# Value products of an attention block issued in runs of two and four head groups, with a fourth slot for the probabilities

## The chip, the core and the metric

The kernel runs on one core of a Trainium2 chip. Its engines work side by side and each takes its own instructions in order: TensorE (PE in the profile, with PEld for its weight loads), VectorE (DVE), ScalarE (ACT), GpSimd (POOL) and SyncE (SP, which issues the DMAs). They wait for one another on semaphores. The metric is the device time of one execution in microseconds (us).

## What is computed

One transformer layer over eight sequences of 256 tokens and width 256: differential attention with 16 heads (two queries a head, so 32 score maps), an added input and a layer norm, then a gated MLP with a router weight, a second added input and a second norm. The part that matters here:

```python
q = jnp.concatenate([q1, q2], axis=1)            # 32 query heads of 16
k2, v2 = jnp.repeat(k, 2, axis=1), jnp.repeat(v, 2, axis=1)
scores = jnp.einsum('bhqd,bhkd->bhqk', q, k2) * scale
p = jax.nn.softmax(jnp.where(causal, scores, finfo.min), axis=-1)
y = jnp.einsum('bhqk,bhkd->bhqd', p, v2)
y = y[:, :H] - sigmoid(x @ Wlam) * y[:, H:]
```

## The kernel before

One iteration handles sequence i of the attention, together with the MLP of sequence i-1 and the end of sequence i-2. The order of each engine's work is written out by hand; nothing reorders it. The first iteration (i = 0) has no MLP in it, the second (i = 1) has no work of sequence i-2, the last (i = 7) has no next sequence to prepare.

The stage that is changed is the one from scores to values. The 32 score maps are split in 8 groups (`GROUPS`). For group g these steps follow one another:

- PE, `t_group(g)` (L746 to L765): three units of transposed scores, u = 0, 1, 2, each into one of four banks (`ring` 0 to 2 and `misc`, taken in turn). A unit waits until the exponentials of the unit four before it are done, since these empty its bank.
- ACT, `exps(g)` (L513 to L518): three exponentials into `prob`, slot g % `RING`, with `RING` = 3. The first one waits, from group 3 on, until the value products that read the slot before are done (`pv_full`).
- POOL, `causal(g)` (L406 to L414): two masks over the slot, one when two exponentials are done, one after the third.
- PE, `pv_group(g)` (L767 to L789): the value products, 16 matmuls of 128*32 in the profile, four next to one another in the columns of the array, into `ybank[g % 2]`. They wait for the masks and for the copy of the group two before.
- DVE, `evacuate_pv(g)` (L1039 to L1041): a copy of the bank to `yv`.

PE's loop in `iteration` issues `t_group(g)`, then for g = 0, 1, 2 a gate/up unit of the MLP (units 4, 5 and 6, `FF_SCORES`; L672 to L674), then from g = 2 on `pv_group(g - 2)`. After the loop come `v_job` (projection of the next values, absent in the last iteration) and `y_jobs` (transposes L800), which wait for the copies to `yv`.

The other engines have MLP work in the same stage. ACT's order is exps(2), tanh of unit 6 (L526), `h_first` of unit 5 (L478), exps(3), `h_first` of unit 6, exps(4), and so on to exps(7). DVE's order is:

```python
for g in range(GROUPS):
    if has_prev and g + 1 in FF_SCORES:
        mlp_unit(i - 1, FF_SCORES[g + 1])
    evacuate_pv(i, g)
    if has_last:
        if g == 0:
            second_norm_start(i - 2, *norm2)
        elif g == SCALE_GROUP + 2:
            second_norm_end(i - 2)
```

So `mlp_unit` of unit 6 (L1030, L1036) stands behind the copy of group 0 and the statistics of the second norm (L999, L1005), and `second_norm_end` (L1126) stands between the copies of groups 5 and 6. POOL has `second_scale` (L386, L388) and the `h_lo` of unit 6 (L403) between the masks of groups 3 and 4.

Two tiles come in with the change. `rest` holds the second half of the split q and k of the next sequence while they are made; `y1` holds the normalized heads, written by DVE after `y_jobs` and read by PE's `yT_job`.

Of the kernel before, what the change touches and what calls it, by code (L numbers as in the profile page):

```python
# [26 lines left out]
B, T, D = 8, 256, 256  # L27
# [10 lines left out]
QK_JOBS = QK_BLOCKS // 2  # L38
# [9 lines left out]
GROUPS = 8  # L48
# [7 lines left out]
LAST_STEPS = 3  # L56
V_COLS = 32
RING = 3
STACKS = 2
X_SLOTS = 3  # L60
REST_SLOTS = 2
HALF = P // 2
# [15 lines left out]
FF_FIRST, FF_MAX, FF_Y0, FF_Y1 = 0, range(1, 4), 7, 8  # L78

FF_SCORES = {0: 4, 1: 5, 2: 6}  # L80
PROJ_CHUNKS = QK_JOBS + 1

SEAM_UNITS = 2
# [4 lines left out]
SCALE = float(HEAD_DIM) ** -0.5  # L88
# [7 lines left out]
ACT = mybir.ActivationFunctionType  # L96
# [3 lines left out]
def build_layer(nc, x, xT, w_proj, w_out, w_gu, w_down, w_router, out):  # L100
    with ExitStack() as ctx:
# [3 lines left out]
        def sem(name):  # L105
# [20 lines left out]
        rest = sb("rest", [P, REST_SLOTS, 2 * T])  # L126
# [7 lines left out]
        max_parts = sb("max_parts", [HEADS * Q_TILES, MAX_PARTS, P], BF16)  # L134
        prob = sb("prob", [P, RING, 3, 2 * T])
        yv = sb("yv", [P, GROUPS, T])

        recip = sb("recip", [P, 3, HEADS])
        y1 = sb("y1", [P, TT, D])
# [9 lines left out]

        gate_t = sb("gate_t", [P, RING, T])  # L150
        h_full = sb("h_full", [P, RING, T])
        h_hi, h_lo = sb("h_hi", [P, FF_UNITS, T], F32R), sb("h_lo", [P, FF_UNITS, T], F32R)
# [14 lines left out]
                     (0, slice(0, yv_cols), yv[:, :, :].rearrange("p g t -> p (g t)")),  # L167
                     (0, slice(yv_cols, gu_cols), mlp_out[:, RING, 0:gu_cols - yv_cols]))

# [30 lines left out]
        qk_full, qk_raw_done, qk_h_done, qk_rest_done, qk_m_done, qk_l_done = (sem(n) for n in ("qk_full", "qk_raw_done", "qk_h_done", "qk_rest_done", "qk_m_done", "qk_l_done"))  # L200
# [4 lines left out]
        t_full, exp_done, causal_done, pv_full, yv_done = (sem(n) for n in ("t_full", "exp_done", "causal_done", "pv_full", "yv_done"))  # L205

        y1_full, y2_full, y1_done, y2_done, y_done = (sem(n) for n in ("y1_full", "y2_full", "y1_done", "y2_done", "y_done"))
        yT_full, yT_hi_done, yT_lo_done, wo_full, z1_done = (sem(n) for n in ("yT_full", "yT_hi_done", "yT_lo_done", "wo_full", "z1_done"))
# [13 lines left out]
        def is_first(b):  # L222
            return b == 0
# [4 lines left out]
        def s_job(u):  # L228
            i, j = S_JOBS[u]
            heads = S_TILE_HEADS[i]  # L230
            return i, range(j * heads, (j + 1) * heads), (i + 1) * HALF

        def t_bank(g, u):
            return score_banks[(3 * g + u) % len(score_banks)]
# [18 lines left out]
        def _(sp):  # L253
# [15 lines left out]
            def load_stacks(b):  # L269
                if b >= STACKS:  # L270
                    sp.wait_ge(t_full, (b - STACKS + 1) * T_UNITS)
                for p in range(3):
# [63 lines left out]
        def _(pool):  # L336
# [69 lines left out]
            def causal(b, groups):  # L406

                for g in groups:
                    first = prob[:, g % RING, 0:2, 0:T].rearrange("p x (i c) -> p x i c", i=2)
                    last = prob[:, g % RING, 2, :].rearrange("p (x i c) -> p x i c", x=2, i=2)  # L410
                    for units, v in ((2, first), (3, last)):
                        pool.wait_ge(exp_done, b * T_UNITS + 3 * g + units)
                        pool.affine_select(out=v, in_=v, compare_op=ALU.is_ge, fill=0.0, base=0,  # L413
                                           pattern=[[0, 2], [HALF, 2], [0, 2], [1, HALF]], channel_multiplier=-1).then_inc(causal_done, 1)  # L414
# [61 lines left out]
        def _(act):  # L476
# [36 lines left out]
            def exps(b, g, units=range(3)):  # L513
                for u in units:
                    act.wait_ge(t_full, b * T_UNITS + 3 * g + u + 1)
                    if u == 0 and g >= RING:
                        act.wait_ge(pv_full, b * GROUPS + g - RING + 1)
                    act.activation(prob[:, g % RING, u, :], t_bank(g, u)[:, :], ACT.Exp, scale=SCALE).then_inc(exp_done, 1)  # L518

            def gate_tanh(b, n):  # L520
                act.wait_ge(gu_full, b * FF_UNITS + n + 1)
# [147 lines left out]
        def _(pe):  # L669
# [76 lines left out]
            def t_group(b, g):  # L746

                rows = slice(0, STACK_ROWS + MAX_PARTS)
                for u in range(3):
                    before = 3 * g + u - len(score_banks)  # L750
                    if before >= 0:
                        pe.wait_ge(exp_done, b * T_UNITS + before + 1)
                    elif g == 0:
                        pe.wait_ge(max_done, b * S_UNITS + S_UNITS - RING + u + 1)
                    else:
                        pe.wait_ge(max_l_done, b + 1)
                    if u < 2:
                        n = 2 * g + u
                        mm = pe.matmul(t_bank(g, u)[:, :], keys_of(b, rows, n, slice(0, P)), q_pair(b, rows, n, slice(0, 2 * T)), start=True, stop=True)  # L759
                    else:  # L760
                        for j in range(2):
                            n = 2 * g + j
                            mm = pe.matmul(t_bank(g, u)[:, j * T:(j + 1) * T], keys_of(b, rows, n, slice(P, T)), q_pair(b, rows, n, slice(T, 2 * T)),  # L763
                                           start=True, stop=True)
                    mm.then_inc(t_full, 1)  # L765

            def pv_group(b, g, has_next):  # L767

                bank = ybank[g % 2]
                if g >= 2:  # L770
                    pe.wait_ge(yv_done, b * GROUPS + g - 1)
                elif has_next:
                    n = (QK_JOBS - 1, 1)[g]
                    pe.wait_ge(qk_raw_done, b * QK_JOBS + n + 1)
                    pe.wait_ge(qk_h_done, (b + 1) * QK_JOBS + n + 1)
                elif g == 0:
                    pe.wait_ge(z1_done, b)
                else:
                    pe.wait_ge(y2_done, b * TT)
                for t in range(TT):  # L780
                    pe.wait_ge(causal_done, b * (2 * GROUPS) + 2 * g + t + 1)
                    for j in range(4):
                        if t == 0:
                            p = prob[:, g % RING, j // 2, :].rearrange("p (i h t) -> p h i t", h=2, t=HALF)[:, j % 2, :, :]
                        else:
                            p = prob[:, g % RING, 2, :].rearrange("p (x i h t) -> p x h i t", x=2, h=2, t=HALF)[:, j // 2, j % 2, :, :]
                        mm = pe.matmul(bank[V_COLS * j:V_COLS * (j + 1), t * P:T], v_ones[:, t, 2 * g + j // 2, :], p,  # L787
                                       start=(t == 0), stop=(t == TT - 1))
                mm.then_inc(pv_full, 1)  # L789
# [119 lines left out]
            def iteration(i, has_next, has_prev, has_last):  # L909
                if i == 2:  # L910
                    pe.wait_ge(mlp_w_lo_done, W_DOWN)
                if not has_prev:
                    first_scores(i)
                for u in range(S_UNITS):
                    if u >= SEAM_UNITS:
                        s_unit(i, u)
                    if has_next and u in QK_AT:
                        qk_job(i + 1, QK_AT.index(u))
                    if has_last and u in SHARED_AT:
                        shared_chunk(i - 2, SHARED_AT.index(u))  # L920
                    if has_prev and u == X1T_AT:
                        x1T_job(i - 1)
                    if has_prev and u == ROUTER_AT:
                        router_job(i - 1)
                    if has_last and u == ROUTED_AT:
                        routed_job(i - 2)
                    if has_prev and u == LOGIT_AT:
                        logit_job(i - 1)
                if has_prev:
                    gu_units(i - 1, (FF_FIRST,))  # L930
                max_job(i, has_prev)
                if has_prev:
                    gu_units(i - 1, FF_MAX)
                pe.wait_ge(max_loaded, (i + 1) * (16 * MAX_PARTS))
                for g in range(GROUPS + 2):
                    if g < GROUPS:
                        t_group(i, g)
                    if g in FF_SCORES and has_prev:
                        gu_units(i - 1, (FF_SCORES[g],))
                    if g >= 2:  # L940
                        pv_group(i, g - 2, has_next)
                if has_next:
                    v_job(i + 1, 0)
                y_jobs(i, 0)
                if has_prev:
                    gu_units(i - 1, (FF_Y0,))
                y_jobs(i, 1)
                if has_prev:
                    gu_units(i - 1, (FF_Y1,))
                yT_job(i)  # L950
                if has_next:
                    v_job(i + 1, 1)
                    first_scores(i + 1)
                wo_job(i)
# [316 lines left out]
```

## Time and profile before

| | before |
|---|---|
| median of 3 runs | 467.77 us (466.49 to 467.85) |
| the profiled execution's own time | 466.94 us |
| its span | 465.2 us, so 1.74 us lie around the span |
| PE busy | 417.3 us, 90% |
| DVE busy | 282.7 us, 61% |
| POOL busy | 244.6 us, 53% |
| ACT busy | 234.9 us, 51% |
| mean granted clock of TensorE | 0.958 |

Shares are means over the whole span. One iteration takes about 51 us; the stage from scores to values is some 17 us of it, and in it the engines are loaded otherwise than in the rest. The chain that ended last is followed back from the last instruction to what released each step, so it shows which engine set the pace where.

### The profile page before, as it was taken

To read this page: it belongs to the slowest core of one execution; us is meant where nothing else is said; L and a number is where in the kernel's file an instruction comes from. 1 tells how busy PE (TensorE), PEld (TensorE's weight loads), DVE (VectorE), ACT (ScalarE), POOL (GpSimd) and SP (SyncE) were. 2 spreads that over 40 slices of the span, in tenths; PEclk is the share of its full clock that TensorE was granted. 3 is DMA by queue.
4 is the path that set the end of the run, shared out by engine and by line. 5 is a ranking of instruction groups with operands and counts; after the bars stand their busy time and mean duration, and the time that the engine had idled before them with its cause. 6 is when DMAs were issued, how large, how long until landed. Compare 5 with 4: busy or idle time off the path is not lost.

```text
span 465.2 us, 10336 instructions
## 1 busy us (share of the span) xinstructions
PE 417.3 (90%) x4008; PEld 339.7 (73%) x4008; DVE 282.7 (61%) x676; ACT 234.9 (51%) x532; POOL 244.6 (53%) x334
## 2 busy tenths in 40 slices
PE   4229697899999999999999999999999999997995
PEld 4127246696799768994998669985898579856995
DVE  3637237753658557764758466755767478747474
ACT  4704481539334853567254944476355922592240
POOL 8314483629355754668254945576365922492152
PEclk9859798979999999999999999999999999999899
DMA  8762770346012810363123610381034410000000
GB/s 284 245 162 63 198 196 2 88 117 151 1 46 85 204 46 4 108 156 69 46 61 108 163 46 25 103 198 33 24 85 112 117 46 0 4 1 25 1 25 23
DMA packets 34753, 40.41 MB, mean 87 GB/s; under 512 B 4240, under 2 KB 28304, under 8 KB 34448
## 3 DMA queue, kind: packets, MB, share of 16 engines
q1 hardware_dynamic: 34704, 39.75, 31.6%
q8 instruction: 32, 0.52, 0.5%
q14 instruction: 17, 0.14, 0.1%
HBM read 27.94 MB, written 11.53 MB: 85 GB/s over the span
## 4 chain that ended last, share of the span: by engine, by line
PE 71%; POOL 9%; DVE 8%; ACT 4%; DMA 3%; issue 2%; SPq 2%; POOLq 0%; DVEq 0%; ACTq 0%
PE ff L672 11%; PE ff L673 10%; PE ff L674 10%; PE ring L735 7%; POOL prob L413 6%; PE ybank L787 5%; PE ybank L672 4%; PE ring L730 4%; PE ring L759 3%; PE ybank L673 3%; PE ybank L674 3%; PE ring L763 2%; ACT prob L518 2%; DVE neg_max L1020 2%; PE ybank L800 2%
## 5 line engine op out<-in xcount | busy, mean ns | idle before, releaser
L1020 DVE TENSOR_REDUCE neg_max<-ring 128x2 f32<-128x512 f32 (+3 forms) x176 | 102.7, 638 | 39.1 <-PE ring L735 38.5
L403 POOL TENSOR_TENSOR h_lo<-h_full,h_hi 128x256 fp32r<-128x256 f32 x72 | 52.9, 735 | 101.6 <-ACT h_hi L478 101.6
L413 POOL TENSOR_SCALAR_AFFINE_SELECT prob<-prob 128x512 f32<-128x512 f32 x128 | 82.9, 679 | 15.6 <-ACT prob L518 14.5
L672 PE MATMUL ff<-x1T_hi,wg_lo 128*128 128x256 f32 x288 | 87.2, 303 | 0.0
L518 ACT ACTIVATE prob<-ring 128x512 f32<-128x512 f32 x144 | 78.3, 620 | 6.9 <-PE ring L759 6.9
L673 PE MATMUL ff<-x1T_lo,wg_hi 128*128 128x256 f32 x288 | 81.2, 282 | 0.0
L674 PE MATMUL ff<-x1T_hi,wg_hi 128*128 128x256 f32 x288 | 81.0, 281 | 0.0
L730 PE MATMUL ring<-mask_b,ident_b 128*128 128x128 bf16 (+2 forms) x176 | 45.4, 258 | 18.9 <-DMA q_stack<-qk_parts_dram 17.1
L1041 DVE COPY yv<-ybank 128x256 f32<-128x256 f32 x64 | 27.0, 422 | 56.9 <-PE ybank L787 56.5
L735 PE MATMUL ring<-k_stack,q_stack 96*128 96x256 bf16 (+3 forms) x512 | 60.9, 239 | 0.0
L787 PE MATMUL ybank<-prob,v_ones 128*32 128x256 f32 (+1 forms) x1024 | 56.3, 335 | 2.0 <-POOL prob L413 1.8
L672 PEld LDWEIGHTS ff<-x1T_hi,wg_lo 128*128 128x128 f32 x288 | 55.0, 191 | 3.3 <-issue 1.3
L526 ACT ACTIVATE gate_t<-ff 128x256 f32<-128x256 f32 x72 | 27.7, 385 | 56.6 <-PE ff L674 56.6
L673 PEld LDWEIGHTS ff<-x1T_lo,wg_hi 128*128 128x128 f32 x288 | 55.1, 191 | 0.0
L674 PEld LDWEIGHTS ff<-x1T_hi,wg_hi 128*128 128x128 f32 x288 | 54.9, 190 | 0.0
L1030 DVE SCALAR_TENSOR_TENSOR gate_t<-gate_t,ff 128x256 f32<-128x256 f32 x72 | 30.0, 416 | 33.5 <-ACT gate_t L526 33.4
L787 PEld LDWEIGHTS ybank<-prob,v_ones 128*32 128x32 f32 x1024 | 25.8, 109 | 29.4 <-issue 9.3
L735 PEld LDWEIGHTS ring<-k_stack,q_stack 96*128 96x128 bf16 x512 | 37.2, 102 | 3.3 <-issue 1.1
L368 POOL TENSOR_TENSOR rest<-rest,parts 128x512 f32<-128x512 f32 x21 | 24.4, 1162 | 28.1 <-ACT parts L478 28.1
L478 ACT ACTIVATE rest<-ybank 128x512 f32<-128x512 f32 x21 | 12.5, 595 | 51.5 <-PE ybank L674 51.5
L730 PEld LDWEIGHTS ring<-mask_b,ident_b 128*128 128x128 bf16 x176 | 17.2, 98 | 27.9 <-issue 17.3
L394 POOL TENSOR_TENSOR parts<-rest,parts 128x512 bf16<-128x512 f32 x24 | 27.8, 1160 | 18.2 <-ACT parts L478 10.2
(169 smaller groups left out, 962.7 us busy)
## 6 DMA issues: line engine op xcount, KB each, us to landing
q_stack<-qk_parts_dram SPq DMA_DIRECT2D x48, 256.0 KB, 4.5
qk_parts_dram<-parts SPq DMA_DIRECT2D x72, 128.0 KB
k_stack<-qk_parts_dram SPq DMA_DIRECT2D x48, 128.0 KB, 4.4
xt_raw<-xT SPq DMA_DIRECT2D x8, 256.0 KB, 2.8
xz<-x SPq DMA_DIRECT2D x8, 256.0 KB, 2.8
out<-xz SPq DMA_DIRECT2D x7, 256.0 KB, 2.2
prob<-w_gu SPq DMA_DIRECT2D x1, 1152.0 KB, 7.3
yv<-w_gu SPq DMA_DIRECT2D x1, 1024.0 KB, 9.1
```

The costliest lines, as they stand in the source:

```text
L394: pool.tensor_tensor(part_order(2, n), psum_order(rest_slot(b, n)), part_order(1, n), ALU.subtract).then_inc(qk_l_done, 1)
L403: pool.tensor_tensor(h_lo[:, n, :], h_full[:, n % RING, :], h_hi[:, n, :].bitcast(F32), ALU.subtract).then_inc(h_lo_done, 1)
L413: pool.affine_select(out=v, in_=v, compare_op=ALU.is_ge, fill=0.0, base=0, pattern=[[0, 2], [HALF, 2], [0, 2], [1, HALF]], channel_multipl ...
L518: act.activation(prob[:, g % RING, u, :], t_bank(g, u)[:, :], ACT.Exp, scale=SCALE).then_inc(exp_done, 1)
L672: pe.matmul(o, lhs_lo, rhs_hi, start=first, stop=False)
L673: pe.matmul(o, lhs_hi, rhs_lo, start=False, stop=False)
L674: return pe.matmul(o, lhs_hi, rhs_hi, start=False, stop=last)
L730: pe.matmul(o[:, :, keys - HALF:keys], ident_b[:, :], mask_b[:, :].unsqueeze(1).to_broadcast([P, len(columns), HALF]), start=True, stop=Fa ...
L735: mm = pe.matmul(o[:, j, :], q_stacks[b % STACKS][rows, row, block, i * P:(i + 1) * P], k_stacks[b % STACKS][rows, row, block, 0:keys], st ...
L787: mm = pe.matmul(bank[V_COLS * j:V_COLS * (j + 1), t * P:T], v_ones[:, t, 2 * g + j // 2, :], p, start=(t == 0), stop=(t == TT - 1))
L1020: dve.tensor_reduce(neg_max[:, columns.start:columns.stop, i], ring[u % RING][:, 0:len(columns) * keys].rearrange("p (h k) -> p h k", k=keys),
L1030: dve.scalar_tensor_tensor(gate_t[:, n % RING, :], gate_t[:, n % RING, :], 1.0, ff[n % 2][:, 0:T], ALU.add, ALU.mult).then_inc(gate_done, 1)
```

## The change

PE's loop issues the value products in three runs: groups 0 and 1 behind the scores of group 3, groups 2 and 3 behind those of group 5, and groups 4 to 7 behind those of group 7. The probabilities get a fourth slot, made of the tile `rest` (the first two units) and the tile `y1` (the third). The first exponential of group g now waits for the value products of group g - 4; in group 3 it also waits until the split of q and k (`qk_l_done`) and the transposes of the sequence before (`yT_full`) are through with the two tiles. The orders of ACT, POOL and DVE stay as they were.

```diff
+PROB_SLOTS = 4
+PV_BEHIND = {3: (0, 1), 5: (2, 3), 7: (4, 5, 6, 7)}
...
+        def prob_first(g):
+            return rest[:, :, :] if g % PROB_SLOTS == RING else prob[:, g % PROB_SLOTS, 0:2, :]
+
+        def prob_last(g):
+            return y1[:, :, :].rearrange("p t d -> p (t d)") if g % PROB_SLOTS == RING else prob[:, g % PROB_SLOTS, 2, :]
+
+        def prob_unit(g, u):
+            return prob_first(g)[:, u, :] if u < 2 else prob_last(g)
...
-                    first = prob[:, g % RING, 0:2, 0:T].rearrange("p x (i c) -> p x i c", i=2)
-                    last = prob[:, g % RING, 2, :].rearrange("p (x i c) -> p x i c", x=2, i=2)
+                    first = prob_first(g)[:, :, 0:T].rearrange("p x (i c) -> p x i c", i=2)
+                    last = prob_last(g).rearrange("p (x i c) -> p x i c", x=2, i=2)
...
-                    if u == 0 and g >= RING:
-                        act.wait_ge(pv_full, b * GROUPS + g - RING + 1)
-                    act.activation(prob[:, g % RING, u, :], t_bank(g, u)[:, :], ACT.Exp, scale=SCALE).then_inc(exp_done, 1)
+                    if u == 0 and g >= PROB_SLOTS:
+                        act.wait_ge(pv_full, b * GROUPS + g - PROB_SLOTS + 1)
+                    if u == 0 and g == RING:
+                        act.wait_ge(qk_l_done, min(b + 2, B) * QK_JOBS)
+                        if not is_first(b):
+                            act.wait_ge(yT_full, b)
+                    act.activation(prob_unit(g, u), t_bank(g, u)[:, :], ACT.Exp, scale=SCALE).then_inc(exp_done, 1)
...
-                            p = prob[:, g % RING, j // 2, :].rearrange("p (i h t) -> p h i t", h=2, t=HALF)[:, j % 2, :, :]
+                            p = prob_unit(g, j // 2).rearrange("p (i h t) -> p h i t", h=2, t=HALF)[:, j % 2, :, :]
...
-                            p = prob[:, g % RING, 2, :].rearrange("p (x i h t) -> p x h i t", x=2, h=2, t=HALF)[:, j // 2, j % 2, :, :]
+                            p = prob_last(g).rearrange("p (x i h t) -> p x h i t", x=2, h=2, t=HALF)[:, j // 2, j % 2, :, :]
...
-                for g in range(GROUPS + 2):
-                    if g < GROUPS:
-                        t_group(i, g)
+                for g in range(GROUPS):
+                    t_group(i, g)
                     if g in FF_SCORES and has_prev:
                         gu_units(i - 1, (FF_SCORES[g],))
-                    if g >= 2:
-                        pv_group(i, g - 2, has_next)
+                    for pv in PV_BEHIND.get(g, ()):
+                        pv_group(i, pv, has_next)
```

## Rows read from the trace of the kernel before

**Rows 1.** Busy us (instructions) by stretch: PE, PEld, DVE, ACT, POOL; clock, DMA, GB/s.

```profile
209.90:220.83 10.93, 10.59 (x150) 4.70 (x149) 5.73 (x15) 8.65 (x19) 9.73 (x16) 1.00 0.26 62
220.83:254.70 33.87, 33.29 (x310) 31.36 (x307) 25.01 (x62) 13.64 (x33) 14.82 (x17) 1.00 0.22 65
```

**Rows 2.** Chain that ended last, iteration 3: start, us, what.

```profile
215.34 4.41 POOL prob L413 x7
219.89 1.01 PE ybank L787 x16
```

**Rows 3.** Timeline of PE, iteration 3: start, us, instruction, idle before and its releaser.

```profile
209.69 0.28 PE L674 MATMUL ff<-x1T_hi,wg_hi 128*128 128x256 f32 x1
209.90 0.86 PE L787 MATMUL ybank<-prob,v_ones 128*32 128x256 f32 x16
210.69 0.60 PE L759 MATMUL ring<-q_stack,k_stack 98*128 98x512 bf16 x2
211.13 0.38 PE L763 MATMUL misc<-q_stack,k_stack 98*128 98x256 bf16 x2
211.44 0.86 PE L787 MATMUL ybank<-prob,v_ones 128*32 128x256 f32 x16
...
214.43 0.39 PE L763 MATMUL ring<-q_stack,k_stack 98*128 98x256 bf16 x2
...
220.83 0.39 PE L672 MATMUL ring<-wp_hi,xt_lo 128*128 128x272 f32 x1
...
221.68 1.03 PE L800 MATMUL ybank<-ident,yv 128*128 128x128 f32 x8
```

**Rows 4.** Timeline of PE's weight loads, iteration 0, one run and two runs together.

```profile
62.81 0.59 PEld L787 LDWEIGHTS ybank<-prob,v_ones 128*32 128x32 f32 x16 [0.21 <-DVE yv L1041]
...
64.36 1.24 PEld L787 LDWEIGHTS ybank<-prob,v_ones 128*32 128x32 f32 x32 [0.21 <-DVE yv L1041]
```

**Rows 5.** Timeline of DVE, iteration 3.

```profile
210.82 0.42 DVE L1041 COPY yv<-ybank 128x256 f32<-128x256 f32 x1 [1.61 <-PE ybank L787]
...
212.53 0.42 DVE L1036 SCALAR_TENSOR_TENSOR h_full<-gate_t,ff 128x256 f32<-128x256 f32 x1
...
218.76 0.42 DVE L1041 COPY yv<-ybank 128x256 f32<-128x256 f32 x1 [1.12 <-PE ybank L787]
...
220.48 0.90 DVE L1041 COPY yv<-ybank 128x256 f32<-128x256 f32 x2
```

**Rows 6.** Timeline of ACT, iteration 3.

```profile
210.29 0.41 ACT L478 ACTIVATE h_hi<-h_full 128x256 fp32r<-128x256 f32 x1
211.12 1.09 ACT L518 ACTIVATE prob<-ring 128x512 f32<-128x512 f32 x2 [0.42 <-PE ring L759]
...
212.98 0.42 ACT L478 ACTIVATE h_hi<-h_full 128x256 fp32r<-128x256 f32 x1 [0.29 <-DVE h_full L1036]
213.31 1.56 ACT L518 ACTIVATE prob<-ring 128x512 f32<-128x512 f32 x3
214.74 0.61 ACT L518 ACTIVATE prob<-misc 128x512 f32<-128x512 f32 x1
```

**Rows 7.** Timelines of DVE, ACT and PE, iteration 1.

```profile
110.09 0.42 DVE L1036 SCALAR_TENSOR_TENSOR h_full<-gate_t,ff 128x256 f32<-128x256 f32 x1
...
111.35 1.59 ACT L518 ACTIVATE prob<-ring 128x512 f32<-128x512 f32 x3
...
118.64 0.39 PE L672 MATMUL ring<-wp_hi,xt_lo 128*128 128x272 f32 x1
```

**Rows 8.** Timelines of DVE and PE, iteration 7.

```profile
420.72 0.90 DVE L1041 COPY yv<-ybank 128x256 f32<-128x256 f32 x2
...
421.27 1.12 PE L800 MATMUL ybank<-ident,yv 128*128 128x128 f32 x8
```

**Rows 9.** Busy time by stretch, end of iteration 7 (columns as in rows 1).

```profile
425.90:429.30 3.40, 1.34 (x10) 0.89 (x9) 2.27 (x6) 1.59 (x4) 1.46 (x2) 1.00 0.00 0
429.30:432.70 3.40, 3.40 (x18) 3.40 (x17) 1.37 (x3) 0.00 (x0) 0.00 (x0) 0.50 0.00 0
```

## The prediction

> **What bounds the kernel now.** I read the page first: PE is busy 90% of the span, the others 51 to 61%. That is a mean over unlike stages, so I went to the busy time by stretch. From the first transposes of one iteration to the last gate/up unit before the values of the next, PE is busy 33.29 of 33.87 us, and in the stage of the change 10.59 of 10.93 [rows 1]. Both look like PE. The chain of waits corrects this for the stage: seven masks of POOL follow one another there without a gap, 4.41 us, and the last value products start when the last mask is through [rows 2]. So PE runs ahead, waits a little at the end, and the pace is set by ACT and POOL, which hand over group by group. The timelines of the single engines then show who waits: ACT has a gap of 0.42 us before exps(3), until the scores of group 3 come from PE, and one of 0.29 us before the `h_hi` of unit 6, until DVE has made `h_full` [rows 6]. DVE itself has waited 1.61 us for the value products of group 0 [rows 5]. These two gaps decide the change. What follows the stage is full of PE, so a delay of the stage goes on to the end undiminished.
>
> **The change part by part.** I take iteration 3 as the pattern of iterations 2 to 6.
>
> *Fewer switches on PE.* A run of value products occupies PE for 0.79 us until the next scores start (209.90 to 210.69) [rows 3]; of two runs back to back the weight loads span 1.24 us against 0.59 for one, so the second costs 0.65 [rows 4]. The way back to full-width scores is thus 0.14 us. Scores take 0.75 us (210.69 to 211.44), and their units follow at 0.22, three of them 0.66, so the way in is 0.09 [rows 3]. Before there are six runs, afterwards three: 3 x 0.23 = 0.7 us of PE an iteration goes away. The Trainium skill, TensorEngine Tiling (Array Packing), section Key Properties, says that a change of tiling mode drains TensorE; the trace agrees with 0.23 us a run. What that page would make of the change stands with the rivals.
>
> *Scores of group 3 ahead of the value products of group 0.* PE is free for them at 209.81 (209.90 less the way in) instead of 210.69. ACT is free at 210.29 + 0.30 = 210.59 (an `h_hi` holds it 0.3: 212.98 to 213.31), so exps(3) starts at 210.59 instead of 211.12: ACT gains 0.53 us [rows 3, 6]. But pv_group(0) now starts 0.75 us of scores after 209.81, at 210.56: 0.66 later.
>
> *Who stands behind pv_group(0).* DVE's copy of group 0 starts 0.92 us after it (209.90 to 210.82), so at 211.48. Behind it in DVE's order stand the norm statistics and `mlp_unit` 6; `h_full` is done at 212.95 now (212.53 + 0.42), then at 213.61 [rows 5]. Behind that, in ACT's order, stand the `h_hi` of unit 6 and all of exps(4): the `h_hi` goes from 212.98 to 213.64, exps(4) from 213.31 to 213.97 [rows 6]. ACT is through with exps(3) at 210.59 + 3 x 0.48 = 212.03 (0.48 is the pitch, 213.31 to 214.74 for three), so it stands 1.6 us where it stood 0.29. The 0.53 is lost, and 0.66 more.
>
> *Scores in pairs.* The second unit of group 5 needs the bank that the first exponential of group 4 empties. A bank is free about 0.64 us after its exponential starts (213.79 to 214.43) [rows 3, 6], so the second unit goes at 214.6 and the third, one pitch on, at 215.09. PE, back at scores at 210.56 + 0.65 + 0.79 = 212.00, is through with those of group 4 at 212.66 and with the first unit of group 5 at 212.88; it stands idle 1.7 us and, before the third unit, 0.25 more. pv_group(2), long ready, stands behind these units; it starts at 215.09 + 0.31 = 215.40. The run of two takes 0.65 + 0.79, so the scores of group 6 start at 216.84, and exps(6) 0.43 us later (210.69 to 211.12) at 217.27. ACT was through with exps(5) at 213.97 + 6 x 0.48 = 216.83: another 0.44 lost. The last unit of group 7 waits for the second exponential of group 6 (217.27 + 0.48 + 0.64 = 218.40), and the run of four starts 0.31 later, 218.71. Four times 0.65 end at 221.31; 0.12 for the copy of group 4, which the third waits for, and 0.14 of way back put `v_job` at 221.57. Before it was 220.83: +0.75 us.
>
> *The tail on DVE.* The copy of group 5 starts at 218.71 + 0.65 + 0.92 = 220.28 (now 218.76); `second_norm_end` follows, so that the copy of group 6 comes 1.72 later, at 222.00 (now 220.48) [rows 5]. The transposes of `y_jobs` need that copy. In iteration 7 they start 0.55 behind it [rows 8]; so at 222.55, where `v_job` alone (0.85) would allow 222.42. Before: 221.68 [rows 3]. The delay is 0.87, and 0.92 in their second half, which needs the copy of group 7. I take 0.9 for each of iterations 2 to 6.
>
> *The other iterations.* In iteration 1 there are no norm statistics: `h_full` goes from 110.51 to 111.17, exps(4) from 111.35 to 111.52, +0.17. From exps(4) to `v_job` it is 118.64 - 111.35 = 7.29 us [rows 7]; by the steps above 221.57 - 213.97 = 7.60. Together +0.5. In iteration 7 no `v_job` covers the copies, so the whole 1.52 us of the copy of group 6 shows: +1.5 [rows 5, 8]. In iteration 0 no MLP work holds up ACT: it gains up to 0.5 from the early scores and loses 0.3 to the pairs; I take 0.
>
> *At nothing.* The new waits of exps(3) are for work that ended in the stages before (POOL's third parts, the transposes of the last sequence); behind it stands all of ACT, but nothing is late. exps(7) waits for pv_group(3) instead of pv_group(4): earlier. No DMA is issued or moved, and SP's order is untouched. Exponentials and masks of groups 3 and 7 use `rest` and `y1`: the trace has no such row. The lower bound is no cost, since shape and engine are the same; the upper is that each exponential takes its whole 0.61 us instead of the pitch of 0.48 [rows 6], where group 3 has cover and group 7 has not: 3 x 0.13 x 8 = +3 us. I take nothing, because the shape is the same. POOL, 0.63 a mask against 0.72 for half of ACT's group, follows ACT; its last mask starts about 220.5, and is over just as the second half of pv_group(7) wants it (221.2).
>
> *Sum.* 0 + 0.5 + 5 x 0.9 + 1.5 = +6.5 us. The profiled execution took 466.94, so 473.4; the median of the runs is 0.83 above it, which makes 474.3 us.
>
> **Rivals.**
>
> A. *PE is the bound after all* (faster). For it: 10.59 of 10.93 us busy [rows 1]. If every unit of scores finds its bank free, the three runs saved pay: 0.7 x 8 = 5.5 us less, 462.3 us. It decides from the point where exps(4) starts no later than 213.3; then the 0.53 us that exps(3) gains must also not be lost at the `h_hi`. Against it: a row already shows ACT waiting there for DVE. The Trainium skill's rule on drains, taken alone, forecasts this case. Chance 0.07.
>
> B. *It comes out even*. The delay at exps(4) is made up, because the copy of group 0 is not what holds DVE, or because POOL gave back what PE loses; the pairs then cost 0.3 in seven iterations less what exps(3) gains, 0 to +1.3 us, 468 to 469. Nothing in the timelines speaks for it but that the first order had 0.3 us of waiting for POOL at its end. Chance 0.07.
>
> C. *The gap on PE also costs clock* (slower still). At the end of iteration 7 PE was busy 1.34 of 3.40 us, and in the next 3.40 us the granted clock was 0.50 of full, 1.2 instead of 2.4 GHz [rows 9]. By my steps PE would be busy about 1.4 us from 212.4 to 215.8. Half the clock for 3.4 us of full work costs at most 1.7. If it falls in two of the five iterations, +3.4: 477.7 us. Against it: the gap is 1.7 and 0.25 us, not one long one, and part of what follows waits for ACT anyway. Chance 0.15.
>
> **Numbers.** The forecast has 0.71: 474.3 us, for itself from 471 (0.4 an iteration and 1 in the last, less than the steps give) to 477 (the 3 us of the tiles' upper bound). With C the range goes to 479; A and B, 0.14, stay below it. Low 470.5, high 479. One measurement of this kernel tells about 0.3% (1.4 us) from no change. Faster 0.07, same 0.07, slower 0.86.
>
> **What would show it.** In iterations 2 to 6: exps(3) earlier by half a microsecond; ACT idle about 1.6 us before the `h_hi` of unit 6, released by DVE `h_full`; PE idle about 1.7 us between the first and second unit of group 5, released by ACT; exps(6) waiting about 0.4 for PE; `y_jobs` behind the copy of group 6; 0.9 us more an iteration; three runs of weight loads at 0.65 a group. If PE is not idle in group 5, A or B holds; if the granted clock of the stage is below 1.00, C does. The prediction is wrong if DVE reaches `mlp_unit` 6 without having waited for the copy of group 0, or if time lost in the stage comes back in the 33.87 us behind it.

## The result and the profile after

The changed kernel takes 474.55 us (median of 4 runs, 473.43 to 478.63), the kernel before 467.81 (4 runs, 466.49 to 469.47). The ratio over the runs is 1.0168, 95% interval 1.0131 to 1.0206; the two medians alone give 1.0144. Ratios here and below go by all runs, save in run 4, where three of six runs that lay over 1.5% above its fastest are left out. The forecast was 474.3. The profiled execution has a span of 471.7 us, 6.5 more than before, at a mean granted clock of 0.954.

The sum is met more closely than its terms. So here is the stage by itself, from the first scores of group 0 to the first transposes of `y_jobs`, the difference of two starts in PE's timeline, for each iteration, in us.

| iteration | 0 | 1 | 2 | 3 | 4 | 5 | 6 | 7 | sum |
|---|---|---|---|---|---|---|---|---|---|
| before | 15.59 | 17.44 | 18.10 | 18.11 | 18.11 | 18.11 | 18.11 | 17.45 | 141.0 |
| after | 15.50 | 17.99 | 20.03 | 18.90 | 18.91 | 18.90 | 20.14 | 18.58 | 148.9 |
| difference | -0.09 | +0.55 | +1.93 | +0.79 | +0.80 | +0.79 | +2.03 | +1.13 | +7.9 |
| forecast | 0 | +0.5 | +0.9 | +0.9 | +0.9 | +0.9 | +0.9 | +1.5 | +6.5 |

All that lies outside these stages is 1.4 us shorter than before. The end alone is 1.6 us shorter: from the transposes of iteration 7 on it takes 42.3 us instead of 43.9. Between the stages nothing of the loss comes back: from the transposes of iteration 3 to the scores of iteration 4 it is 32.96 us before and 33.00 after.

Iteration 3 after, PE's timeline (start, us, instruction, idle before and its releaser). The iteration begins at 205.95 instead of 203.57, so 2.38 us are to be taken off when it is set beside the forecast.

```profile
205.95 0.61 PE L774 MATMUL ring<-q_stack,k_stack 98*128 98x512 bf16 x2
...
212.94 1.51 PE L802 MATMUL ybank<-prob,v_ones 128*32 128x256 f32 x32
214.38 0.60 PE L774 MATMUL ring<-q_stack,k_stack 98*128 98x512 bf16 x2
...
215.04 0.38 PE L774 MATMUL misc<-q_stack,k_stack 98*128 98x512 bf16 x1
216.98 0.39 PE L774 MATMUL ring<-q_stack,k_stack 98*128 98x512 bf16 x1 [1.56 <-ACT prob L533]
217.47 0.39 PE L778 MATMUL ring<-q_stack,k_stack 98*128 98x256 bf16 x2
...
221.12 2.26 PE L802 MATMUL ybank<-prob,v_ones 128*32 128x256 f32 x48
...
224.00 0.39 PE L687 MATMUL ring<-wp_hi,xt_lo 128*128 128x272 f32 x1
```

Two runs of value products now stand together (x32) and take 1.44 us until scores follow, where one took 0.79 [rows 3]. Then PE is idle for 1.56 us before the second unit of group 5, and the releaser is ACT. `v_job` comes at 224.00, less 2.38 at 221.62, where it came at 220.83.

ACT in the same stretch:

```profile
212.97 1.08 ACT L533 ACTIVATE rest<-ring 128x512 f32<-128x512 f32 x2
...
216.03 0.42 ACT L489 ACTIVATE h_hi<-h_full 128x256 fp32r<-128x256 f32 x1 [1.49 <-DVE h_full L1050]
216.35 1.55 ACT L533 ACTIVATE prob<-ring 128x512 f32<-128x512 f32 x3
...
219.66 0.60 ACT L533 ACTIVATE prob<-ring 128x512 f32<-128x512 f32 x1 [0.29 <-PE ring L774]
```

The gap of 0.42 before exps(3), which write `rest` here, is gone; the one before the `h_hi` of unit 6 has grown from 0.29 to 1.49 us [rows 6], released by DVE's `h_full`; and before exps(6) there is a new one of 0.29, for PE.

DVE in the same stretch:

```profile
213.87 0.42 DVE L1055 COPY yv<-ybank 128x256 f32<-128x256 f32 x1 [2.27 <-PE ybank L802]
...
215.57 0.42 DVE L1050 SCALAR_TENSOR_TENSOR h_full<-gate_t,ff 128x256 f32<-128x256 f32 x1
...
222.70 0.42 DVE L1055 COPY yv<-ybank 128x256 f32<-128x256 f32 x1 [0.23 <-PE ybank L802]
223.04 1.01 DVE L1140 TENSOR_SCALAR xz<-xz,ln_mv,ln_t 128x256 f32<-128x256 f32 x2
223.97 0.74 DVE L1055 COPY yv<-ybank 128x256 f32<-128x256 f32 x2
```

It stands 2.27 us before the copy of group 0, where it stood 1.61 [rows 5]: the 0.66 that pv_group(0) is later. The chain that ended last no longer goes through POOL's masks in this stage [rows 2] but through just this:

```profile
213.01 0.83 PE ybank L802 x16
213.87 0.42 DVE yv L1055
214.29 0.67 DVE ln_stats L1013 x2
...
215.57 0.43 DVE h_full L1050
...
216.83 0.60 ACT prob L533
```

The stages of iterations 2 and 6, at 20 us, are something else. Busy time by stretch (columns as in rows 1): iterations 3 and 6 of the kernel after; two stretches inside its iteration 2; and the two stretches behind iteration 7 that lie as far behind its transposes as those of [rows 9] did, in the second of which the clock was at half before.

```profile
206.04:224.94 18.90, 17.10 (x204) 11.18 (x204) 8.21 (x22) 14.77 (x33) 15.06 (x24) 1.00 0.46 116
361.87:382.02 20.15, 18.49 (x204) 11.83 (x204) 8.21 (x23) 14.78 (x33) 15.11 (x24) 0.92 0.44 110
...
162.40:165.84 3.44, 1.78 (x27) 0.98 (x31) 1.02 (x4) 2.84 (x7) 2.94 (x5) 0.99 0.01 4
165.84:169.25 3.41, 3.41 (x22) 1.17 (x14) 0.70 (x2) 2.52 (x7) 2.17 (x4) 0.51 0.00 0
...
434.03:437.43 3.40, 1.38 (x11) 0.93 (x10) 2.21 (x6) 1.59 (x4) 1.45 (x2) 1.00 0.00 0
437.43:440.83 3.40, 3.40 (x33) 3.40 (x32) 1.70 (x5) 0.00 (x0) 0.39 (x2) 1.00 0.00 0
```

The same 204 matmuls take PE 1.4 us longer in iteration 6, at a mean clock of 0.92. In iteration 2 the clock is at 0.51 of full, so at 1.2 instead of 2.4 GHz for nearly all of it, in the stretch that follows PE's gap. And the half clock behind iteration 7 did not come in this execution: 33 matmuls pass in the 3.40 us in which 18 passed before. That is the 1.6 us that the end gained.

### The profile page after: what moved, and what is told of

Read it like the earlier page. It is cut to its first block, busy times and chain, and to the rows that moved or that the text cites. A ratio compares the mean times of both kernels' runs of the same rounds, so it can differ in the third digit from the quotient of the medians.

```text
span 471.7 us, 10336 instructions
## 1 busy us (share of the span) xinstructions
PE 412.1 (87%) x4008; PEld 340.0 (72%) x4008; DVE 278.2 (59%) x676; ACT 234.8 (50%) x532; POOL 246.0 (52%) x334
## 4 chain that ended last, share of the span: by engine, by line
PE 73%; DVE 11%; ACT 6%; DMA 3%; issue 3%; SPq 2%; POOL 1%; POOLq 0%; DVEq 0%; ACTq 0%
PE ff L687 11%; PE ff L688 10%; PE ff L689 10%; PE ybank L802 9%; PE ring L750 7%; ACT prob L533 4%; PE ring L745 4%; PE ybank L687 3%; PE ring L774 3%; PE ybank L689 3%; PE ybank L688 3%; PE ring L778 2%; DMA q_stack<-qk_parts_dram 2%; DVE neg_max L1034 2%; PE ybank L815 2%
## 5 line engine op out<-in xcount | busy, mean ns | idle before, releaser
L424 POOL TENSOR_SCALAR_AFFINE_SELECT prob<-prob 128x512 f32<-128x512 f32 x96 | 62.8, 678 | 18.8 <-ACT prob L533 17.0
L533 ACT ACTIVATE prob<-ring 128x512 f32<-128x512 f32 x112 | 62.0, 609 | 7.9 <-PE ring L774 7.9
L774 PE MATMUL ring<-q_stack,k_stack 98*128 98x512 bf16 x96 | 34.8, 406 | 13.4 <-ACT prob L533 10.0
L802 PE MATMUL ybank<-prob,v_ones 128*32 128x256 f32 (+1 forms) x768 | 37.4, 332 | 0.0
```

The costliest lines, as they stand in the source:

```text
L533: act.activation(prob_unit(g, u), t_bank(g, u)[:, :], ACT.Exp, scale=SCALE).then_inc(exp_done, 1)
```

## The experiments

Each kernel was timed in turns with the kernel before on the same chip; the medians of before lay between 467.89 and 468.48 us.

**1. Unit 6 ahead of the copy, in the changed kernel.** One edit on DVE:

```diff
-                    if has_prev and g + 1 in FF_SCORES:
-                        mlp_unit(i - 1, FF_SCORES[g + 1])
+                    if has_prev and g == 0:
+                        for n in (FF_SCORES[1], FF_SCORES[2]):
+                            mlp_unit(i - 1, n)
                     evacuate_pv(i, g)
```

> The changed kernel with one thing moved on DVE: unit 6 of the MLP ahead of the copy of group 0. Theory (the loss is DVE's unit 6, and with it ACT's exps(4), queued behind the copy of the late value products): exps(4) starts about 1.5 us earlier, PE's gap in group 5 goes, the stage of iterations 3 to 5 shrinks from 18.9 to about 17.6 us (18.11 before the change), and the time is about 465 us, below the kernel before. Rival (the pairs and their banks hold PE, wherever DVE stands): stage at 18.7 or more, 473 us. Rival (the clock lost in PE's gap is the loss): only the two slow iterations recover, about 472 us.

Measured: 464.65 us, ratio to before 0.9935 (0.9910 to 0.9959). The stages of iterations 2 to 6 take 17.54 or 17.55 us, all five, against 18.90 with the change and 18.11 before. DVE's timeline in iteration 3 of this kernel:

```profile
211.66 0.42 DVE L1050 SCALAR_TENSOR_TENSOR h_full<-gate_t,ff 128x256 f32<-128x256 f32 x1
212.27 0.42 DVE L1055 COPY yv<-ybank 128x256 f32<-128x256 f32 x1 [0.19 <-PE ybank L802]
```

ACT's timeline behind it:

```profile
212.80 0.44 ACT L489 ACTIVATE h_hi<-h_full 128x256 fp32r<-128x256 f32 x1
213.21 1.58 ACT L533 ACTIVATE prob<-ring 128x512 f32<-128x512 f32 x3
```

And PE's, the first two units of group 5:

```profile
213.44 0.38 PE L774 MATMUL misc<-q_stack,k_stack 98*128 98x512 bf16 x1
213.86 0.39 PE L774 MATMUL ring<-q_stack,k_stack 98*128 98x512 bf16 x1
```

DVE has made `h_full` while it would have waited, ACT goes from exps(3) to exps(4) without a gap, and PE issues the second unit of group 5 0.42 us behind the first instead of 1.94. The same runs on PE, the same pairs, and the sign of the change turns. The theory holds; both rivals fall.

The edit takes unit 6 past the copy and also past the norm statistics behind it. Iteration 1 of the changed kernel has no statistics, and there ACT's gap is 0.57 us instead of 1.49, and the stage loses 0.55 instead of 0.79:

```profile
111.02 0.42 ACT L489 ACTIVATE h_hi<-h_full 128x256 fp32r<-128x256 f32 x1 [0.57 <-DVE h_full L1050]
```

Run 3 below, without the pairs, loses 0.28 in that iteration. So the late copy alone is enough for a loss, and what else stands between the copy and unit 6 adds to it.

**2. The same edit in the kernel before.**

> The kernel before with the same move on DVE alone. Theory: there the h_hi of unit 6 waited only 0.29 us and POOL's masks set the end of the stage, so nothing changes: stage 18.1 us, 467.8 us. Rival (any gain of the first run is simply the better order on DVE): about 465 us here too.

Measured: 467.89 us, ratio 0.9999 (0.9975 to 1.0023), stages of 18.12 us. The chain that ended last goes through POOL's masks in iteration 3, as in the kernel before:

```profile
217.55 4.42 POOL prob L413 x7
```

The better order on DVE is worth nothing here by itself; it is needed only once the value products are late.

**3. Late, but one by one.** The changed kernel with

```diff
-PV_BEHIND = {3: (0, 1), 5: (2, 3), 7: (4, 5, 6, 7)}
+PV_BEHIND = {3: (0,), 4: (1,), 5: (2,), 6: (3,), 7: (4, 5, 6, 7)}
```

> The changed kernel with runs of one: groups 0 to 3 one by one behind the scores of groups 3 to 6, groups 4 to 7 behind group 7. The lateness of group 0 is kept, the pairs are undone. Theory (lateness is most of it, pairs the rest): stage of iterations 2 to 6 about 0.6 us above the kernel before, 472 us. Rival (the pairs are the loss): 467.8 us. Rival (drains are worth their 0.23 us a run): two runs more than the changed kernel, so slower than it, 475 us or more.

Measured: 471.82 us, ratio 1.0098 (1.0063 to 1.0133). The undisturbed stages take 18.63 us: 0.52 above before, and 0.27 below the changed kernel. So lateness is two thirds of the 0.79, the pairs one third (the last run of four is the same in both). Iteration 4 took 20.20, with a clock of 0.92 in its stage. PE of iteration 3 shows the same gap, a little shorter, between the first two units of group 5:

```profile
213.00 0.39 PE L774 MATMUL misc<-q_stack,k_stack 98*128 98x512 bf16 x1
214.71 0.39 PE L774 MATMUL ring<-q_stack,k_stack 98*128 98x512 bf16 x1 [1.32 <-ACT prob L533]
```

**4. Both edits.**

> Both edits: runs of one, one group late, and unit 6 first on DVE. Theory: the early scores of group 3 now pay and nothing is queued behind the late copy; iterations 2 to 6 gain 0.5 us each against the kernel before until POOL's masks hold the end, 464.5 us, as much as the first run or a little more, although there are two more runs on PE. Rival (drains): 0.5 us an iteration slower than the first run.

Measured: a median of 465.23 us (459.11 to 466.28), ratio 0.9869 (0.9812 to 0.9926). The stages say it more plainly: 17.58 us, against 17.54 in the first run. The chain that ended last, iteration 3 of this kernel:

```profile
211.45 3.78 POOL prob L424 x6
215.23 0.64 POOL rest L424
...
216.00 1.01 PE ybank L802 x16
```

Two runs of value products more on PE, 0.46 us by [rows 3, 4], make no difference here: POOL's masks end this stage. That is less than a proof that switches are free, since run 1 ends otherwise: its chain goes through ACT's exponentials and through PE's run of two (1.44 us) and run of four (3.03), with no mask of POOL in it. The two stages come out alike with different ends. The rival that puts the weight on the drains falls for run 4. What the Trainium skill states in TensorEngine Tiling (Array Packing), Key Properties, that a change of mode drains the array, is not touched by this. The 0.23 us a run are there in PE's rows, only not on this path.

**5. The fourth slot alone.** The new tiles and waits, with PE's order as before (`PV_BEHIND = {2: (0,), 3: (1,), 4: (2,), 5: (3,), 6: (4,), 7: (5, 6, 7)}`).

> The order of the kernel before on PE (runs as they were), with the fourth slot in the other two tiles and the new waits. Theory: the tiles and the waits cost nothing, stage 18.1 us, 467.8 us. Rival (exponentials and masks in the other tiles are dearer, up to 0.4 us an iteration): 468 to 471 us, stage 18.2 to 18.5.

Measured: 467.78 us, ratio 0.9998 (0.9974 to 1.0022), stages of 18.11 to 18.12 us. The tiles and the waits cost nothing that the stage shows.

**6. PE's gap filled.** The changed kernel with spare products, whose results are thrown away, behind the first unit of group 5:

```diff
+                    if g == 5 and u == 0 and not is_first(b):
+                        pe.wait_ge(yv_done, b * GROUPS + 1)
+                        for _ in range(12):
+                            pe.matmul(ybank[0][:, 0:T], wg_hi[:, 0, 0:P], x1T_hi[:, 0, :], start=True, stop=True)
```

> The changed kernel with twelve spare matmuls of 256 columns (1.4 us, results thrown away) in PE's gap between the first and second unit of group 5, from iteration 1 on. Theory (the gap makes the clock fall in some iterations): no iteration at half clock in the stage, 18.9 us in all of iterations 2 to 6 instead of up to 20.1, about 0.8 us more in iteration 1 whose gap is shorter, 472 to 473 us with less scatter than the changed kernel. Rival (the two slow iterations have nothing to do with the gap): slow iterations of 20 us stay, 474 us or more. Rival (the gap is not idle for want of ACT): the spare matmuls push the stage out by up to 1.4 us, 480 us.

Measured: 474.76 us, ratio 1.0158 (1.0126 to 1.0190). Iterations 2 to 6 took 18.92, 18.91, 18.86, 18.91 and 18.91: no stage at a lower clock in this execution, and none of the five pushed out by the spare work. PE's timeline in iteration 3 of this kernel, the spare matmuls and the second unit of group 5:

```profile
214.35 1.76 PE L784 MATMUL ybank<-x1T_hi,wg_hi 128*128 128x256 f32 x12
216.27 0.39 PE L774 MATMUL ring<-q_stack,k_stack 98*128 98x512 bf16 x1
```

The time as a whole is not clearly shorter: iteration 1 pays 0.34 more, iteration 7 had the half clock behind it again (43.9 us from its transposes to the end), and the runs scatter as before. My 472 to 473 was too low.

**7. The changed kernel a second time.**

> The changed kernel as it is, a second look. Theory (whether the clock falls in PE's gap depends on where the gap lies in time, not on the iteration): undisturbed stages of 18.9 us again, with stages near 20 us in other iterations than 2 and 6, or in another number of them; time 473 to 478 us, as that number goes. Rival (iterations 2 and 6 are slow for a reason of their own): the same two at 20 us.

Measured: 476.53 us (6 runs), ratio 1.0173 (1.0144 to 1.0202). Undisturbed stages of 18.9 again, and about 20 now in iterations 3, 6 and 7. Busy time by stretch, iterations 3 and 4:

```profile
205.50:225.50 20.00, 18.34 (x204) 11.90 (x203) 8.14 (x23) 14.78 (x33) 15.15 (x24) 0.91 0.44 111
258.50:277.40 18.90, 17.11 (x204) 11.16 (x203) 8.28 (x23) 14.78 (x33) 15.17 (x24) 1.00 0.46 117
```

So it is not the iteration. Over all the profiled executions here, a full iteration (2 to 6) fell to a lower clock in 5 of 15 stages with the gap open (the changed kernel twice, and run 3), in none of the 35 in which the gap was not there, and in none of the 5 in which it was filled. Five stages are few: at one in three, all five stay clear by luck in one case of eight. The clock of the other executions says more. With the gap filled, the mean granted clock was 0.954 or 0.958 in all 5; in the changed kernel it was 0.945 to 0.948 in 7 of 10. So the idle time itself is likely what costs the clock; the total time does not show it.

**8. POOL's item last.** Run 4, and on POOL the `h_lo` of unit 6 behind the last mask:

```diff
-                    if has_prev and g - 1 in FF_SCORES:
+                    if has_prev and g - 1 in FF_SCORES and g < 3:
                         n = FF_SCORES[g - 1]
                         h_rests(i - 1, range(n, n + 1))
                 if has_prev:
-                    h_rests(i - 1, range(FF_Y0, FF_UNITS))
+                    h_rests(i - 1, range(FF_SCORES[2], FF_UNITS))
```

> Runs of one, one group late, unit 6 first on DVE, and on POOL the h_lo of unit 6 behind the last mask instead of between the masks of groups 3 and 4. Theory (POOL's 0.68 us there hold the masks, and through them the end of the stage): stage of iterations 2 to 6 at about 17.2 us, 462 us, below the fourth run. Rival (ACT holds the end already): 17.6 us, as the fourth run.

Measured: 461.03 us, ratio 0.9832 (0.9794 to 0.9870): the fastest of all by its median, 7.2 us below that of before in the same rounds. Stages of 17.03 us, a little shorter than forecast. POOL's timeline in iteration 3 of this kernel, with the masks straight behind the scale of the second norm, 10.51 us into the stage where they came at 11.18 in run 4:

```profile
214.41 0.71 POOL L399 TENSOR_TENSOR ln_t<-ln_t,minus_half 128x2 f32<-128x2 f32 x1
215.08 3.82 POOL L424 TENSOR_SCALAR_AFFINE_SELECT prob<-prob 128x512 f32<-128x512 f32 x6
```

The busy time of that stage (columns as in rows 1):

```profile
204.57:221.60 17.03, 17.03 (x204) 11.14 (x203) 8.56 (x23) 14.56 (x33) 15.01 (x24) 1.00 0.56 133
```

PE is busy for all of the 17.03 us, and the chain that ended last holds nothing but PE from the scores of group 3 on. In iteration 3 of every other kernel here the chain leaves PE for ACT, DVE or POOL; here, and only here, PE is the bound of the stage. Whether the three runs of the change would pay here was not run.

**9. The two moves without the change.** The kernel before with the edits of runs 1 and 8.

> The kernel before with the two moves on DVE and POOL and nothing of the change. Theory: with POOL's item out of the way the old order gains too, but keeps its late scores of group 3: stage 17.5 us, 464.5 us, between the kernel before and the run with the scores early. Rival (the gain of the early scores was POOL's all along): the same 17.2 us as that run.

Measured: 464.02 us, ratio 0.9924 (0.9895 to 0.9953), stages of 17.52 us. Of the 1.08 us that run 8 gains in an iteration, 0.59 come without the change, and 0.49 with the later value products. In iteration 3 of run 9 ACT still waits for the scores of group 3, and the chain goes from there through POOL's masks:

```profile
210.68 1.08 ACT L518 ACTIVATE prob<-ring 128x512 f32<-128x512 f32 x2 [0.42 <-PE ring L759]
```

So most of the 0.49 is what the early scores save. The later value products also make one run less, which is not on this chain.

## Why the prediction was right, and where only the sum was

**The stall.** Taken 2.38 us back, the steps of iteration 3 lie where they were put: exps(4) at 213.97 (forecast 213.97), the run of two at 215.41 (215.40), the scores of group 6 at 216.85 (216.84), exps(6) at 217.28 (217.27), the run of four at 218.74 (218.71), `v_job` at 221.62 (221.57). ACT's gap was 1.49 us where 1.6 was forecast, PE's 1.56 where 1.7 was, and the wait of exps(6) 0.29 where 0.44 was. All three were forecast a little too long because I let an engine be free one pitch after its last instruction started (0.48 on ACT, 0.22 on PE), while that instruction itself takes 0.61 or 0.38 [rows 3, 6]; the starts, which carry the sum, do not depend on it. (For exps(6) there is a slip besides: 213.97 + 6 x 0.48 is 216.85, not 216.83.) Run 1 shows that this is the cause and not only the order in which things happened: with `mlp_unit` 6 off the queue behind the copy, the loss of 0.79 becomes a gain of 0.57. Run 3 shows the split between lateness and pairs.

**The tail was too dear.** I took 1.72 us from the copy of group 5 to that of group 6, as before [rows 5]; it took 1.27, because `second_norm_end` took 1.01 us instead of 1.46. Its row before, for the one shown above:

```profile
219.11 1.46 DVE L1126 TENSOR_SCALAR xz<-xz,ln_mv,ln_t 128x256 f32<-128x256 f32 x2
```

So the copies are not what `y_jobs` waits for in iterations 2 to 6, `v_job` is: 0.79 instead of 0.9 each. In iteration 7 the term was 1.13 instead of 1.5. Undisturbed, the stages add up to -0.09 + 0.55 + 5 x 0.79 + 1.13 = 5.54 us, not 6.5.

**The clock made up for it.** What rival C described came as well, in two of five iterations, as in its example: +1.1 and +1.2 us, less than the 1.7 each that I had as the most. At the end the half clock of before was missing, 1.6 us less. These three and +0.2 us elsewhere make +0.94, and the forecast total is met by that. It is luck of this execution: in the profiled execution of run 7 three stages fell and the end was at half clock too, and the median of that run was 476.53. The likeliest case and C should not have been set apart as they were; with a gap of 1.3 to 1.6 us the clock fell in 5 of 15 stages.

**The rest.** The tiles and waits at nothing: right (run 5). POOL off the path in the changed kernel: right, the chain has none of its masks in the stages of iterations 1 to 7. The iterations 0 and 1: right. Rivals A and B: neither holds, and A needed more than a free `mlp_unit`: even then the stage ended through ACT (run 1), and two runs more cost nothing where POOL ended it (run 4).

## What to carry to other kernels

Moving a product later on one engine moves what reads it on the next, and then everything that stands behind that reader in its own queue, also work that has nothing to do with it. Before a reordering, write down for each moved step who waits for it and what stands behind the waiter; here one call on DVE, moved ahead of a copy, made the difference between 1.7% slower and 0.7% faster. And before saving work on the engine that looks busiest, see from the chain who ends the stage: where POOL's masks ended it, 0.46 us of switches more on PE cost nothing (run 4), and 0.7 us of POOL's work moved behind the masks bought half a microsecond an iteration (run 8).

## What the runs showed of the hardware

*DVE beside POOL.* The two `tensor_scalar` of `second_norm_end` (128x256, f32) took 785 and 751 ns in iteration 3 before, while POOL's masks ran; after the change the first took 694, beside a mask, and the second, with POOL idle, 396. POOL before, then after:

```profile
215.29 5.12 POOL L413 TENSOR_SCALAR_AFFINE_SELECT prob<-prob 128x512 f32<-128x512 f32 x8
...
222.91 0.68 POOL L424 TENSOR_SCALAR_AFFINE_SELECT y<-y 128x512 f32<-128x512 f32 x1
```

All 14 of the kernel before, by source line (durations in ns as min/median/max, first and last start):

```profile
L1126 DVE TENSOR_SCALAR xz<-xz,ln_mv,ln_t x14: 406/751/785, 168.0 to 449.2; 128x256 f32<-128x256 f32 x14
```

The same of the kernel after:

```profile
L1140 DVE TENSOR_SCALAR xz<-xz,ln_mv,ln_t x14: 395/404/694, 171.2 to 455.7; 128x256 f32<-128x256 f32 x14
```

A duration is thus also a matter of what runs beside it, and moves with the order. The Trainium skill, SBUF — State Buffer, section SBUF: two separate sides, says that DVE, in some of its instructions, and GpSimd share a pair of ports which one of them holds for a whole instruction; the trace agrees that these are longer beside a mask, and does not show how. Not all work of POOL did this: the last two of the kernel before, at 448.8 us, began beside an `h_lo` (L403, 448.35 to 449.09) and took 406 and 444 ns.

*The clock after a short gap.* In iteration 2 of the changed kernel the granted clock fell to half although PE was idle for no longer than 1.56 us at a stretch; it had been busy 1.78 of the 3.44 us before the fall. In run 3 it fell in iteration 4, with a gap of 1.31 us. In which iteration it fell changed from one execution to the next.
